# A graph network on one core: one gathered tile in thirty-two is taken from the transposed features, column by column, on VectorE

## The reference, cut to what matters

```
# layer 0
msg   = relu(x[dst] @ Wd + x[src] @ Ws + edge_attr @ We + ...)      # one row of 128 for each edge
agg   = segment_sum(msg, dst)
x     = layernorm(x + relu(concat(x, agg, u) @ W2.T + b2))
# layer 1
h     = relu(x[src] @ Ws' + x[dst] @ Wd' + edge_attr @ We' + b)
mean  = segment_mean(h, dst) @ msg_w2 + b2
x     = layernorm(x + relu(concat(x, mean) @ upd_w1 + b1) @ upd_w2 + b2)
```

## Time and profile before

| | us |
|---|---|
| median of three timed runs | 4714.24 |
| the three runs | 4712.52, 4714.24, 4715.95 |
| span of the profiled execution | 3929.8 |
| what the median has above that span | 784.4 |

### The profile page before, as it was taken

One profiled execution on the slowest core, in us unless ns is written; L12 is line 12 of the kernel. 1 busy time (PEld: TensorE's weight loads), 2 busy tenths in 40 slices (PEclk: granted clock), 3 DMA queues, 4 the chain that ended last, 5 costly groups with the idle time before them and its releaser, 6 DMA issues.

```text
span 3929.8 us, 45222 instructions
## 1 busy us (share of the span) xinstructions
PE 3229.0 (82%) x16881; PEld 2975.7 (76%) x16881; DVE 1583.8 (40%) x3640; ACT 590.4 (15%) x1017; POOL 2960.2 (75%) x3156
## 2 busy tenths in 40 slices
PE   6988888888788888888878888878888888888887
PEld 6877777777777777777778777777777777777776
DVE  6533334343444444444543333333433333333333
ACT  1211111111111111111111111111111111111111
POOL 7777777777777777777777777777777777777776
PEclk7755555565655556665665555555555555555556
DMA  7644444444444444445454444444444444444443
GB/s 261 200 138 134 135 136 143 132 133 139 148 139 149 149 149 147 147 147 154 131 158 135 133 131 124 135 139 136 139 136 141 139 142 137 140 135 141 142 142 100
DMA packets 257760, 563.18 MB, mean 143 GB/s; under 512 B 131254, under 2 KB 151713, under 8 KB 232572
## 3 DMA queue, kind: packets, MB, share of 16 engines
q1 hardware_dynamic: 132824, 332.20, 25.4%
q0 software_dynamic: 100032, 205.00, 19.8%
q10 hardware_dynamic: 24676, 23.01, 1.7%
HBM read 537.29 MB, written 22.66 MB: 142 GB/s over the span
## 4 chain that ended last, share of the span: by engine, by line
POOL 70%; issue 23%; DMA 4%; DVE 2%; PE 2%; ACT 0%; SPq 0%; POOLq 0%; DVEq 0%
POOL Qr L319 70%; DMA Qr<-tabQ,srcE 3%; DVE BIG L1405 1%; PE bank L1137 0%; DMA srcE<-in_srcL 0%; DVE BIG L1302 0%; PE bank L1119 0%; PE bank L1092 0%; DVE BIG L1392 0%; DMA tabQ<-BIG 0%; DVE BIG L1400 0%; PE bank L1051 0%; PE bank L1045 0%; DVE AC L609 0%; POOL Qr L325 0%
## 5 line engine op out<-in xcount | busy, mean ns | idle before, releaser
L319 POOL DMA_INDIRECT Qr<-tabQ,srcE x3094 | 2925.3, 945 | 942.9 <-issue 933.2
L1137 PE MATMUL bank<-BIG 128*128 128x42 f32 x6252 | 1379.0, 396 | 143.6 <-ACT BIG L1287 141.1
L1119 PE MATMUL bank<-wall,BIG 128*128 128x128 f32 x6252 | 1473.0, 410 | 19.1 <-DMA BIG<-tabP 19.1
L1137 PEld LDWEIGHTS bank<-BIG 128*128 128x128 f32 x6252 | 1307.5, 308 | 207.6 <-ACT BIG L1287 201.5
L1302 DVE TENSOR_TENSOR BIG<-bank,BIG 126x512 bf16<-126x512 f32 x782 | 539.3, 690 | 2264.7 <-DMA Qr<-tabQ,srcE 2254.8
L1119 PEld LDWEIGHTS bank<-wall,BIG 128*128 128x128 f32 x6252 | 1311.5, 309 | 23.8 <-issue 23.8
L1287 ACT ACTIVATE BIG<-BIG 128x512 f32<-128x512 f32 (+1 forms) x782 | 492.1, 629 | 3229.1 <-DVE BIG L1405 3220.4
L1124 PE MATMUL bank<-BIG 126*128 126x128 bf16 x3126 | 490.2, 295 | 506.5 <-DVE BIG L1302 396.7
L1124 PEld LDWEIGHTS bank<-BIG 126*128 126x128 bf16 x3126 | 342.0, 135 | 639.0 <-DVE BIG L1302 455.9
L1405 DVE TENSOR_TENSOR BIG<-bank,Qr 128x512 f32<-128x512 f32 (+1 forms) x782 | 532.7, 681 | 41.2 <-PE bank L1124 25.3
L1392 DVE TENSOR_TENSOR BIG<-bank,relE 128x168 f32<-128x168 f32 x782 | 252.6, 323 | 3.5 <-DMA Qr<-tabQ,srcE 3.5
(11 more groups left out here) (137 smaller groups left out, 609.9 us busy)
## 6 DMA issues: line engine op xcount, KB each, us to landing
BIG<-in_eaT SPq DMA_DIRECT2D x194, 1024.0 KB, 5.4
BIG<-in_dstR SPq DMA_DIRECT2D x194, 504.0 KB
Qr<-tabQ,srcE POOLq DMA_INDIRECT x3094
BIG<-tabP SPq DMA_DIRECT2D x526, 31.5 KB
tabP<-BIG ACTq DMA_DIRECT2D x22, 384.0 KB, 3.1
tabQ<-BIG ACTq DMA_DIRECT2D x17, 256.0 KB, 5.2
X<-in_xN SPq DMA_DIRECT2D x1, 3136.0 KB, 16.8
tabE<-BIG ACTq DMA_DIRECT2D x11, 256.0 KB, 2.3
```

The lines of the kernel that those rows point to most:

```text
L319: e.indirect_dma_start(Q[0:p, i % R_Q, j, :], None, table[:, :], bass.IndirectOffsetOnAxis(ap=srcE[0:p, g, j:j + 1], axis=0)).then_inc(f_q ...
L1119: e.matmul(bank[i % R_C][:, j * D:(j + 1) * D], f_eaT[:, k % R_EA, (g % LQ * J + j) * P:(g % LQ * J + j + 1) * P], wc[l], start=(j == 0), ...
L1137: last = e.matmul(sums[:, 0:W], M[:, i % R_M, j, :], S[:, hot(i), j, :], start=(j == 0 and first_of(i)), stop=(j == n - 1 and last_of(i)))
```

## The change

In every eighth group GpSimd gathers three tiles instead of four. The 128 source rows of the fourth are built otherwise. VectorE copies, for each of its 128 edges, the source's column of `XT` into one column of a block `XC` (two blocks of 128 by 128). It does so 16 columns at a time, in the eight steps from 12 to 5 ahead of the group's own, with one register load of 16 node numbers ahead of each 16 copies. TensorE multiplies the block by `Ws` straight into the group's bank. The table in DRAM isn't read for these edges. VectorE's sum L1405 then covers three tiles, and ScalarE takes the fourth tile's relu from the bank in a second instruction.

The groups are 16, 24, ... 120 in layer 0 (14 of them, as long as `XT` still holds the old features) and 16, 24, ... 384 in layer 1 (47 of them). So 61 gathers go, and 488 steps of VectorE get 16 copies each, 7808 in all.

```diff
 LAST = BASE[-1]
+
+PIECES = 8
+PIECE = P // PIECES
+COL_AT = 4
+LEAD = 12
+COLS = [[i for i in range(COL_AT + LEAD, NG - 2, PIECES) if l or i - LEAD + PIECES - 1 < DUE[0]["second"][0]] for l in range(2)]
+R_X = 2
+
+
+def col_tile(i):
+    l, g = divmod(i, NG)
+    return len(COLS[0]) * l + COLS[l].index(g) if l < 2 and g in COLS[l] else None
+
+
+def col_group(k):
+    return COLS[0][k] if k < len(COLS[0]) else NG + COLS[1][k - len(COLS[0])]
 
...
 
+        def gathered(i):
+            return tiles(i % NG) - (col_tile(i) is not None)
+
         def q_count(i):
-            return 16 * sum(tiles(x % NG) for x in range(i % R_Q, i + 1, R_Q))
+            return 16 * sum(gathered(x) for x in range(i % R_Q, i + 1, R_Q))
 
...
                     e.wait_ge(fs["tt"], i - R_Q + 1)
-                for j in range(tiles(g)):
+                for j in range(gathered(i)):
                     p = VP if g == NG - 1 and j == VJ else P
...
             e.dma_start(basE, a["base"].broadcast_to([P, NGP])).then_inc(s_bas, 16)
+            e.dma_start(colI[0:len(COLS[1]), :], a["srcC"]).then_inc(s_bas, 16)
             e.dma_start(cb[:, :], a["rows"][:, 3 * D:4 * D].broadcast_to([P, D])).then_inc(s_cb, 16)
...
         p1 = {n: sem(f"p1_{n}") for n in ("c", "hi", "r", "mid", "lo")}
+        s_col = gs[1]["bt"]
         s_mz, s_mean, s_ind, s_u, s_ru, s_meet = (sem(n) for n in ("s_mz", "s_mean", "s_ind", "s_u", "s_ru", "s_meet"))
...
                             e.matmul(bank[i % R_C][:, j * D:(j + 1) * D], f_eaT[:, k % R_EA, (g % LQ * J + j) * P:(g % LQ * J + j + 1) * P], wc[l], start=(j == 0), stop=False)
+                        if (c := col_tile(i)) is not None:
+                            e.wait_ge(s_col, PIECES * (c + 1))
+                            e.matmul(bank[i % R_C][:, (J - 1) * D:J * D], XC[:, c % R_X, :], wq[l], start=False, stop=False)
                         e.wait_ge(v_st, i + 1)
...
                         e.wait_ge(v_tt, i + 1)
-                        m = M[:, i % R_M, 0:tiles(g), :].rearrange("p j d -> p (j d)")
-                        e.activation(m, m, ACT.Relu).then_inc(v_rl, 1)
+                        m = M[:, i % R_M, 0:gathered(i), :].rearrange("p j d -> p (j d)")
+                        last = e.activation(m, m, ACT.Relu)
+                        if col_tile(i) is not None:
+                            last = e.activation(M[:, i % R_M, J - 1, :], bank[i % R_C][:, (J - 1) * D:J * D], ACT.Relu)
+                        last.then_inc(v_rl, 1)
 
...
                 e.tensor_tensor(fP3[:, c % R_U, 0:n, 2 * D:3 * D], row_bank(c), fP3[:, c % R_U, 0:n, D:2 * D], ALU.subtract).then_inc(p0["lo"], 1)
+
+            def columns(l, n, q):
+                k = l * len(COLS[0]) + n
+                if q == 0 and k >= R_X:
+                    e.wait_ge(v_C, col_group(k - R_X) + 1)
+                if l == 1 and n == 0 and q == 0:
+                    e.wait_ge(u_tc, NU)
+                _, at = nc.values_load_multi_w_load_instructions(
+                    colI[n:n + 1, q * PIECE:(q + 1) * PIECE], engines=[mybir.EngineType.DVE], min_val=0, max_val=N - 1,
+                    skip_runtime_bounds_check_because="the source of an edge, which is a node")
+                for c in range(PIECE):
+                    last = e.tensor_copy(XC[:, k % R_X, q * PIECE + c:q * PIECE + c + 1], XT[:, bass.ds(at[c], 1)])
+                last.then_inc(s_col, 1)
 
...
                             e.wait_ge(f_q[i % R_Q], q_count(i))
-                        n = tiles(g - 1)
+                        n = gathered(i)
                         e.tensor_tensor(M[:, i % R_M, 0:n, :].rearrange("p j d -> p (j d)"), bank[i % R_C][:, 0:n * D],
...
                                         ALU.add).then_inc(v_ag, 1)
+                    if g >= COL_AT and (g - COL_AT) // PIECES < len(COLS[l]):
+                        columns(l, *divmod(g - COL_AT, PIECES))
                     if l == 0:
```

More of the change, by code:

```diff
@@ L169, in build @@
         srcR = sb("srcR", [P, RAW * J], I32)
+        colI = sb("colI", [P, P], I16)
+        XC = sb("XC", [P, R_X, P])
         vsum = sb("vsum", [P, 1])
@@ L467, in bases_to_rows @@
             def bases_to_rows():
-                e.wait_ge(s_bas, 32)
+                e.wait_ge(s_bas, 48)
                 link(e.tensor_reduce(wrow[:, :], third[:, :], AX, ALU.add))
@@ L625, in general_gpsimd @@
                 for r in range(PF):
-                    e.wait_ge(f_q[r], 16 * J)
+                    e.wait_ge(f_q[r], 16 * gathered(r))
             e.sem_inc(q["done"], 1)
@@ L1585, in laid_out @@
         "srcL": srcp.astype(_np.int32).reshape(NGP, J, P).transpose(2, 0, 1).reshape(P, NGP * J),
+        "srcC": srcp.astype(_np.int16).reshape(NGP, J, P)[COLS[1], J - 1],
         "dstL": dstp.astype(_np.int32).reshape(NGP, J, P).transpose(2, 0, 1).reshape(P, NGP * J),
```

## The result

The changed kernel takes **4840.7 us** against 4715.1: 2.6% slower (ratio 1.0258, interval 1.0235 to 1.0281). I had forecast 4636 and faster. Its profiled execution took 4843 us with a span of 4841.2, so almost nothing lies outside a span. The 784 us between the first profile of the kernel before and its timed runs were therefore no start or end.

A forecast was written before the change was run, and what follows sets the result against it. GpSimd's gathers, 1.249 us each, were taken as the bound: 76.2 us saved less 5 for the port gives 71 off the span, 3859 us. Carried to timed runs, 4643 or 4629, middle 4636 us; range 4618 to 4735.

The forecast's parts named there:

- 306 + 15 x 12.3 = 0.49 us: VectorE's load of 16 registers per step: 306 ns for one value, 12.3 ns for each more, 0.49 us in all.
- In this count the copies cost no time: VectorE's sequencer with load and copies: a step of 3.2 to 3.6 us, below the gathers' 4.84, so no time added.
- 16 x 0.166: VectorE's 16 pairs of register operation and copy per step: 0.166 us each (bounds 0.07 and 0.22), 2.66 us together.
- The overlap: VectorE's sequencer runs ahead of the engine, so the load and first pairs hide under 2 us of wide instructions.
- The rival of a VectorE without overlap: Register operations wait for VectorE's earlier instructions: 5.18 us a step against 4.84, 166 us back, 4804 us; chance 0.19.
- 61 gathers, 76.2 us: GpSimd's chain: 61 gathers of 1.249 us removed, 76.2 us saved.
- The shared port, 5 us: VectorE's copies delaying GpSimd through their shared port: 1891 gathers beside copies at 0.003 us each, 5 us lost.
- TensorE and ScalarE at nothing: 61 more matmuls (25 us) on TensorE, covered by its spare 0.66 us a group, and 61 more ScalarE activations: no cost.
- I take the middle: Timed median 784.4 us above the span: if fixed 4643 us, if proportional (1.20) 4629; the middle, 4636, is the forecast.

The follow-up runs named there:

- 32-bit form: The changed kernel with its node numbers as 32-bit instead of 16-bit integers: 3854.6 us against 3929.2 (ratio 0.9809); beside a kernel before of 4759.8 us, 4822.5 (1.0136).

## Why the prediction was wrong, step by step

- **"306 + 15 x 12.3 = 0.49 us" for the load** is the first of two steps that failed: the load took 3.59 us, seven times as much. I drew a line through two points, one and four 32-bit values that start at a multiple of 16 bytes, and carried it to sixteen 16-bit values. Four such values together cost hardly more than one, so the line says nothing of the next four. Sixteen 32-bit ones would have been 1.11 us, sixteen 16-bit ones are 3.6. I gave the pair of instructions two bounds and this load none, though no row showed it. With 3.6 us in my own count the sequencer's step is 3.6 + 0.05 + 2.66 = 6.3 us, over the 4.84, and the sign turns.
- **"In this count the copies cost no time"** is the second. It took VectorE's spare from a trace in which the gathers pace every step, and the forecast was for runs in which TensorE and gaps in issue do (read from the profile of 4762 us; none was taken of the kernel before at 4714). It holds where the kernel before takes 3929 us (3854.6 with copies and cheap loads, 3853.9 without). Beside 4760 us the same 32-bit form takes 150 us more than the mere drop of the gathers and ends 1.4% slower than the kernel before. The changed kernel's ratio is only 1.2% higher than that, 57 us, as far as ratios of two sets can be compared. So in the runs that the forecast was for, the dear load is the smaller part of the miss.
- **"16 x 0.166"** for the pairs: measured 0.115 us a pair where the gathers set the pace, 1.84 us for 16. Within the bounds, on the safe side.
- **The overlap**: right. The load starts 0.06 us after L1331, under the wide instructions. The rival of a VectorE without overlap was the wrong mechanism for the right sign: VectorE did become the bound of the steps with copies, through the load. Its 4804 us lies near 4841 by chance.
- **61 gathers, 76.2 us**: right, 75.3 measured alone (3929.2 to 3853.9).
- **The shared port, 5 us**: nearer to nothing. In the 32-bit form a gather beside copies comes every 1.249 us, as before, and takes 945 ns. What the Trainium skill says in "SBUF — State Buffer", section "SBUF: two separate sides", of an fp32 `tensor_copy` that keeps GpSimd from its descriptors is not seen for copies of one element; the wide instructions of the earlier trace rows agree with it.
- **TensorE and ScalarE at nothing**: right where the kernel before takes 3929 us, by the run that only drops the gathers.
- **"I take the middle"** of a fixed and a proportional 784 us: as sizes neither is refuted, since beside 4760 us the mere drop gains 87 us (66 to 105), where a fixed difference gives 76 and a proportional one 92. As pictures both are wrong. The timed runs that I compared with were of another kind than the profile, with issue gaps on TensorE and waits of GpSimd that the trace I read hasn't got. In them the bound that I had read off the profile is not the only one. The changed kernel loses 2.6% there and 12.6% where my profile does apply. That what sets these gaps off is tied to the chip is a guess: the sets with 3929 us ran on three chips and those with 4758 and more on three others. What they are stays open.

## What to carry to other kernels

On VectorE, registers loaded from SBUF want 32-bit values, a start at a multiple of 16 bytes, and counts that are multiples of four; a load of sixteen 16-bit values costs three times the 32-bit one and can make a half idle engine the bound, out of sight of its busy time. When a kernel's median lies far above the span of its profile, profile it again before anything is predicted from its rows: the rows may belong to another pace. And a piece of work moved to an idle engine as many small instructions is cheap only while instructions reach that engine without gaps: the same 7808 copies cost nothing in one kind of timing, and with their loads 150 us in the other.

## What the runs showed that I had not expected

- **The price of a register load on VectorE.** All medians fit, within 0.16 us, 0.09 us, plus 0.256 for each four 32-bit values from a multiple of 16 bytes, plus 0.23 for each value besides: one value 0.31 (0.32 by the rule), 4 values 0.34 (0.35), 16 values 1.11 (1.11), 19 values 1.81 (1.80), 22 values 1.82 to 1.86 (1.83), 24 values 1.62 (1.63, said before the run), 18 off the multiple 4.18 (4.23), 22 off it 5.09 (5.15), 16 off it 3.65 and 16 of 16 bits 3.61 (3.77), four of 16 bits 0.95 (1.01).
- **Copies of one column by register** follow each other every 0.115 us on VectorE, with a register operation of 46 ns between them, and leave the gathers beside them at 1.249 us where these set the pace.
- **Gaps, mostly of 0.7 us and multiples from start to start,** in the issue of TensorE's and VectorE's instructions, some 1000 us in all on L1119 and L1137 in the kernel before of 4760 us, and none in the one of 3929 us.
